# Second attention of a two-attention block: products in every second slot, feed-forward steps in the others

## What is computed

```python
x = x + attn_a(layernorm(x))     # 16 heads of 16; softmax over keys, summed: 'blmh,blhd->blhd'
x = x + ffn(layernorm(x))
x = x + attn_b(layernorm(x))
x = x + ffn(layernorm(x))

def attn_b(x):                   # the second attention
    q = (x @ Wq + bq).reshape(b, h, dh, t)      # dh = 16, t = 2048
    k = (x @ Wk + bk).reshape(b, h, dh, t)
    v = (x @ Wv + bv).reshape(b, h, dh, t)
    attn = softmax(einsum('bhdt,bhds->bhts', k, v) * temperature)   # over s
    return einsum('bhdt,bhts->bhds', q, attn).reshape(b, t, d)

def ffn(x):
    y = square(relu(x @ W_fc.T)) @ W_proj.T     # 256 -> 1024 -> 256
    # five steps of a spiking neuron on y; the result is the share of steps with a spike
```

## Time and profile before

| | before |
|---|---|
| median of 3 runs | 3005.08 (3004.95 to 3009.67) |
| the profiled execution | 3006.15, span 3003.9 |
| busy, TensorE / VectorE / ScalarE / GpSimd | 2439.2 / 2547.5 / 2552.0 / 1220.3 |
| mean granted clock of TensorE | 0.947 |
| reductions of the second attention (L805) | 1024, mean 1216 ns |
| exponentials of the second attention (L949) | 1024, mean 1119 ns |
| product matmuls (L560) | 4096 records, mean 605 ns |

### The profile page before, as it was taken

One profiled execution on the slowest core, in us unless ns is written; L12 is line 12 of the kernel. 1 busy time (PEld: TensorE's weight loads), 2 busy tenths in 40 slices (PEclk: granted clock), 3 DMA queues, 4 the chain that ended last, 5 costly groups with the idle time before them and its releaser, 6 DMA issues. The chain is left out here.

```text
span 3003.9 us, 47095 instructions
## 1 busy us (share of the span) xinstructions
PE 2439.2 (81%) x12608; PEld 1045.7 (35%) x12608; DVE 2547.5 (85%) x2612; ACT 2552.0 (85%) x4737; POOL 1220.3 (41%) x1856
## 2 busy tenths in 40 slices
PE   6832777777777777777776999999999999999997
PEld 3400334433334433334433233333333333333333
DVE  5552999999999999999983999999989988998994
ACT  2252999999999999999984999999999999999994
POOL 0000355554455554455543234443344334433444
PEclk9965999999999999999986999999999999999999
DMA  5897111111111111111111111101110111111100
GB/s 170 170 158 86 23 39 32 34 33 37 38 38 32 33 32 38 38 38 31 34 30 44 36 43 40 41 26 42 39 41 27 39 39 41 31 36 40 40 26 13
DMA packets 183490, 138.99 MB, mean 46 GB/s; under 512 B 91012, under 2 KB 170374, under 8 KB 183431
## 3 DMA queue, kind: packets, MB, share of 16 engines
q1 hardware_dynamic: 183430, 138.28, 20.1%
HBM read 92.04 MB, written 41.94 MB: 45 GB/s over the span
## 5 line engine op out<-in xcount | busy, mean ns | idle before, releaser
L805 DVE TENSOR_REDUCE nmax<-score 128x1 f32<-128x1024 f32 x1024 | 1214.1, 1216 | 165.9 <-PE score L580 149.0
L823 DVE TENSOR_REDUCE nmax<-score 128x1 f32<-128x1024 f32 x1024 | 1192.9, 1214 | 172.6 <-PE score L612 167.7
L949 ACT ACTIVATE big<-score,nmax 128x1024 f32<-128x1024 f32 x1024 | 1138.5, 1119 | 124.6 <-DVE nmax L805 118.0
L969 ACT ACTIVATE score<-score,nmax 128x1024 f32<-128x1024 f32 x1024 | 1118.6, 1098 | 127.5 <-DVE nmax L823 126.5
L612 PE MATMUL score<-big,shared 128*128 128x512 bf16 x2048 | 648.8, 406 | 370.8 <-ACT score L969 275.8
L580 PE MATMUL score<-shared 128*128 128x512 bf16 x2048 | 620.0, 390 | 103.7 <-ACT big L949 80.0
L560 PE MATMUL bank_g<-big,qw 128*32 128x512 f32 x4096 | 544.8, 605 | 2.3 <-POOL qw L1123 1.3
L612 PEld LDWEIGHTS score<-big,shared 128*128 128x128 bf16 x2048 | 135.6, 100 | 691.7 <-ACT score L969 549.1
L580 PEld LDWEIGHTS score<-shared 128*128 128x128 bf16 x2048 | 138.6, 98 | 650.0 <-ACT big L949 521.1
L1065 POOL TENSOR_TENSOR hid<-hid 128x512 f32<-128x512 f32 x128 | 133.0, 1039 | 509.0 <-ACT hid L915 509.0
L535 PEld LDWEIGHTS bank_f<-xnT,w_fc_sb 128*128 128x128 f32 x2048 | 295.1, 197 | 78.0 <-ACT hid L915 24.5
(11 more groups left out here) (113 smaller groups left out, 1606.0 us busy)
## 6 DMA issues: line engine op xcount, KB each, us to landing
shared<-q_parts SPq DMA_DIRECT2D x256, 64.0 KB, 3.1
shared<-kb_parts SPq DMA_DIRECT2D x256, 64.0 KB, 2.2
shared<-vb_parts SPq DMA_DIRECT2D x256, 64.0 KB, 2.2
big<-k_parts SPq DMA_DIRECT2D x32, 256.0 KB, 12.5
big<-k_parts SPq DMA_DIRECT2D x8, 1024.0 KB, 56.2
q_parts<-big SPq DMA_DIRECT2D x24, 256.0 KB, 3.1
k_parts<-big SPq DMA_DIRECT2D x24, 256.0 KB, 3.6
kb_parts<-shared SPq DMA_DIRECT2D x96, 64.0 KB, 1.5
```

The costliest lines, as they stand in the source:

```text
L805: v.tensor_reduce(nmax[:, par, c // NCH, c % NCH:c % NCH + 1], score[buffers_b[CPT * par + c][0]][:, :], AX.X, ALU.max, negate=True).then_ ...
L823: v.tensor_reduce(nmax[:, par, c // NCH, c % NCH:c % NCH + 1], score[buffers_a[CPT * par + c][0]][:, :], AX.X, ALU.max, negate=True).then_ ...
L949: a.activation(expo[:, c // NCH, (c % NCH) * CH:(c % NCH + 1) * CH], score[buffers_b[CPT * par + c][0]][:, :], ACT.Exp, bias=nmax[:, par, ...
L969: a.activation(s[:, :], s[:, :], ACT.Exp, bias=nmax[:, par, c // NCH, c % NCH:c % NCH + 1], accum_out=esum[:, par, c // NCH, c % NCH:c % N ...
```

## The change

The slots of phase_b are laid out anew: the products stand in every even slot, one feed-forward step in each odd slot from 3 on (two down steps in slot 31). ScalarE's copies and relus move with them, the copy of the product to the slot of the last product; VectorE's statistics go from slots 24 and 25 to 27 and 28, its last-tile neuron from 22 to 31. There are two qw tiles, so weigh_q waits for the half before the last. The exponentials wait for the products that free their rows at four slots instead of two. GpSimd's list has a new order, with the second square between half_distance and half_sums of half 0.

```diff
-UP_A, UP_B = [18, 19, 20, 21, 22, 23, 24, 25], [4, 4, 5, 5, 8, 11, 14, 14]
-DOWN_A, DOWN_B = [26, 26, 27, 27, 28, 29, 30, 30], [17, 18, 18, 19, 19, 20, 20, 21]
-PROD_AT = [6, 7, 9, 10, 12, 13, 15, 16], [22, 23, 25, 26, 28, 29, 31, 32]
+UP_A, UP_B = [18, 19, 20, 21, 22, 23, 24, 25], [3, 5, 7, 9, 11, 13, 15, 17]
+DOWN_A, DOWN_B = [26, 26, 27, 27, 28, 29, 30, 30], [19, 21, 23, 25, 27, 29, 31, 31]
+PROD_AT = [6, 8, 10, 12, 14, 16, 18, 20], [22, 24, 26, 28, 30, 32, 34, 36]
...
+E_FREE = [(0, 3), (6, HALF), (16, HALF + 4), (24, H)]
...
-        qw = sb("qw", [P, NCH, HALF, 2 * DH])
+        qw = sb("qw", [P, 2, NCH, HALF, 2 * DH])
...
-                    last = mm(bank_g[32 * sc:32 * sc + 32, :], qw[:, sc * BANK // CH, n, :],
+                    last = mm(bank_g[32 * sc:32 * sc + 32, :], qw[:, half, sc * BANK // CH, n, :],
...
-            v.memset(qw[:, :, :, :], 0.0).then_inc(consts, 1)
+            v.memset(qw[:, :, :, :, :], 0.0).then_inc(consts, 1)
...
-                        if c == 24:
+                        if c == 27:
                             ffn_stats_of(T + i1, 1 - par, x3_ready, i1 + 1)
-                        if c == 25:
+                        if c == 28:
                             ffn_mean(T + i1)
-                    if c == 22 and i2 is not None and last_tile(T + i2):
+                    if c == 31 and i2 is not None and last_tile(T + i2):
...
-                    need(act, prod_done, H * (i - 1) + HALF)
-                if c == CPT // 2:
-                    need(act, prod_done, H * i)
+                for at_c, n in E_FREE:
+                    if c == at_c:
+                        need(act, prod_done, H * (i - 1) + n)
...
-                    if i1 is not None and c == PROD_AT[0][-1] + 1:
+                    if i1 is not None and c == PROD_AT[0][-1]:
                         keep_product(i1)
                     if i2 is not None:
                         if c == 1:
                             ffn_columns(T + i2)
-                        if c == 4:
+                        if c == 8:
                             ffn_act(T + i2, 0)
-                        if c == 13:
+                        if c == 16:
                             ffn_act(T + i2, 1)
-                        if c == 20:
+                        if c == 30:
                             ffn_take(T + i2, par)
...
-                need(pool, prod_done, HALF * n)
+                need(pool, prod_done, HALF * (n - 1))
...
-                    last = g_.tensor_tensor(qw[:, c, :, 0:DH].rearrange("p (r m) j -> p r m j", m=KC),
+                    last = g_.tensor_tensor(qw[:, half, c, :, 0:DH].rearrange("p (r m) j -> p r m j", m=KC),
```

More of the change, by code:

```diff
@@ L1217, in phase_b @@
                     half_sums(i1, 1 - par, 1)
-                if i3 is not None:
-                    spikes(T + i3, T - 1 + i3, 1 - par, 7, 8)
                 if i1 is not None:
@@ L1222, in phase_b @@
                 if i3 is not None:
-                    spikes(T + i3, T - 1 + i3, 1 - par, 9, LIF_OPS)
+                    spikes(T + i3, T - 1 + i3, 1 - par, 1, 5)
                 if i2 is not None:
@@ L1226, in phase_b @@
                 if i3 is not None:
+                    spikes(T + i3, T - 1 + i3, 1 - par, 6, 7)
+                if i is not None:
+                    half_distance(i, par, 0)
+                if i2 is not None:
+                    square(T + i2, 1)
+                if i is not None:
+                    half_sums(i, par, 0)
+                if i3 is not None:
+                    spikes(T + i3, T - 1 + i3, 1 - par, 8, 8)
+                if i is not None:
+                    weigh_q(i, par, 0)
+                if i3 is not None:
+                    spikes(T + i3, T - 1 + i3, 1 - par, 9, LIF_OPS)
                     if isinstance(i3, int) and i3 < 2:
@@ L1230, in phase_b @@
                     result(T + i3, T - 1 + i3, 1 - par, out_stored[1 - par], 8 * (i3 - (1 - par)))
[L1231 to L1236, removed]
                 if i1 is not None:
                     add_attention(i1, 1 - par)
-                if i2 is not None:
-                    spikes(T + i2, T - 1 + i2, par, 1, 2)
-                if i1 is not None:
                     normalise(T + i1, 0, ffn_mv, ffn_step, xn[:, :], xin[:, 1 - par, :], ffn_tr, T + i1).then_inc(ffn_xn, 1)
-                if i2 is not None:
-                    spikes(T + i2, T - 1 + i2, par, 3, 6)
                 if i is not None:
```

## The result

| | before | after |
|---|---|---|
| median of 5 runs each, one chip | 3005.31 (3004.95 to 3009.67) | 3025.24 (3024.10 to 3028.96) |
| ratio after / before | | 1.0065 (1.0050 to 1.0079) |
| the profiled execution | 3006.15, span 3003.9 | 3027.4, span 3025.3 |
| copy of the product to the next copy, regular / with the turn-back | 42.03 / 42.49 | 42.97 / 43.35 |

The changed kernel is slower by 19.9, 0.65%. The forecast was slower, by 36.9, at 3042; 3025.24 lies in its range. In the kernel after, lines of phase_b stand two lower: scores L582, products L562, exponential L951, copy of the product L939, reciprocal L798, tot L1113, square L1067, xnT L911.

What follows compares the result with a forecast made beforehand. A ring of TensorE, ScalarE and VectorE was taken as the bound. 0.22 - 1.10 + 1.13 + 1.00 = +1.25 an iteration, mean 1.23 with the turn-back, 36.9 in thirty, gave 3042 by the median; range 3008 to 3053.

Steps and rivals of the forecast that it cites:

- P0 to P8: From the start of slot 0's score matmul (P) to slot 8's: 11.42 against 11.20 before, a loss of 0.22.
- Spacing the products: Products alternating with steps on TensorE: gain 1.10 an iteration in slots 8 to 17, loss 0.22 in slots 0 to 8.
- the release behind xnT: Slot 3's up step on TensorE, taken to start 0.60 after ScalarE's xnT copy starts, at 5.13.
- The square before the sums: GpSimd's second square ahead of half_sums: slot 18's reciprocal on VectorE waits 1.2, loss 1.13 an iteration.
- The copy of the product: Slot 22's product on TensorE waits 1.27 for ScalarE's copy after exponential 20, loss 1.00 an iteration.
- The floor of 1.0: Slot 22's wait for the copy would still be 1.0 if ScalarE stood as close to TensorE as it can.
- both waits: Main case: slot 18's reciprocal and slot 22's product both wait, 3034 to 3050, chance 0.62.
- the sums alone: Rival: only slot 18's reciprocal waits for tot, the copy is hidden: +0.6 an iteration, 3025, chance 0.10.
- clock unchanged: Sign expected in the profile after: the granted clock, 0.99 over the second attention's stretch, stays as it was.
- The ramp and the tail: Start and end of the second attention: ramp 0, between -2 and +1; tail 0, between -3 and +3.
- Neither new wait bites: Rival: in slots 18 to 23 copy and sums are in time: -0.43 an iteration, 2992, chance 0.12.
- The copy alone: Rival: only slot 22's product waits, GpSimd taking relu 1 early: +0.1 an iteration, 3009, chance 0.04.

Runs made afterwards that it cites:

- e2_sums_first: The changed kernel with GpSimd's half_sums of the first half ahead of the second square: 2998.39, ratio 0.9961.
- e9_all_but_slots: The kernel before with two qw tiles, the finer waits and GpSimd's new order, all slots as they were: 3005.63, ratio 0.9995.
- e1_copy_early: The changed kernel with ScalarE's copy of the product one slot earlier, after exponential 19 instead of 20: 3000.21, ratio 0.9966.
- e3_both: The changed kernel with the copy of the product one slot earlier and half_sums ahead of the second square: 2972.24, ratio 0.9876.
- a0_changed: The changed kernel itself, run once more on another chip: 3026.92, ratio 1.0058 to the kernel before.
- e4_both_xnt: The changed kernel with the product's copy one slot earlier, half_sums before the second square, and xnT copied after exponential 0 instead of 1: 2953.11, ratio 0.9812.
- e8_before_slot2: The kernel before with half 0's last product in slot 34 instead of 32, two qw tiles and the finer waits: 3000.78, ratio 0.9974.
- e10_before_xnt: The kernel before with only xnT copied after exponential 0 instead of 1: 3012.78, ratio 1.0006.
- e5_copy_late: The changed kernel with the copy of the product one slot later, after exponential 21 instead of 20: 3078.06, ratio 1.0228.

## Why the prediction was right in its sign and too large

By its own checkpoints, from the scores' starts above:

| stretch | before | predicted | after | predicted change | change |
|---|---|---|---|---|---|
| P0 to P8 | 11.20 | 11.42 | 11.32 | +0.22 | +0.12 |
| P8 to P18 | 13.15 | 12.05 | 12.06 | -1.10 | -1.09 |
| P18 to P22 | 4.96 | 6.09 | 6.00 | +1.13 | +1.04 |
| P22 to next P0 | 12.72 | 13.72 | 13.60 | +1.00 | +0.88 |
| iteration | 42.03 | 43.28 | 42.98 | +1.25 | +0.95 |

**Spacing the products** was right: the ten slots from 8 cost 12.06, in turns of 1.53 and 0.88. Slots 0 to 8 were over by 0.10, and the term that was off is the release behind xnT. Exponential 1 and xnT start 3.43 and 4.53 behind P0, exactly as in the working; the up step starts at 4.96 and not at 5.13. The two rows are, kernel before (TensorE) and kernel after (ScalarE):

```profile
2152.95 0.60 PE L580 MATMUL score<-shared 128*128 128x512 bf16 x2 [0.53 <-ACT big L949]
```
```profile
2162.10 0.37 ACT L911 ACTIVATE xnT<-bank_f 128x256 f32<-128x256 f32 x1
```

My 0.60 from xnT to the step (2152.79 to 2153.39) was no release: in the kernel before, TensorE was still waiting for slot 4 until 2152.95, and the step stands 0.44 behind those scores, which is the length of a score alone. In the kernel after, where TensorE does wait for xnT, it is 0.43 from start to start, 0.06 from the end of the copy. The transposes' slot is 0.69 (2159.09 to 2159.78) where I had 0.80, but that is not on the path: TensorE waits 0.60 in slot 3 all the same.

**The square before the sums** was right in mechanism and place, with 1.07 of idle for 1.2. The relu came 1.19 behind P18 and the square 0.66 behind the relu, where I had 1.23 and 0.70; that is the 0.09 of this stretch. e2_sums_first shows that it is this order, with the new slots, and e9_all_but_slots that it is not the order alone.

**The copy of the product** was right too. Its start came where it was put, 0.97 behind P22 (0.98 in the working), and the product 1.70 behind P22 for 1.80: without the wait it would start at 0.53, so by starts the wait is 1.17 for 1.27 (the record's 1.10 counts from the end of the scores). The step that was off is again the release: I took 0.23 from the copy's end to the product, out of the same misread row on xnT; it is 0.14 (2188.51 to 2188.65). The floor of 1.0 does not follow from my own prices, which give 1.90 + 1.92 - 1.53 - 0.88 - 0.54 = 0.87; e2_sums_first has 0.92 by starts (2176.32 - 2174.87 - 0.53).

**The sum** was mis-sized by a quarter: 0.90 for 1.23 on the mean of the two kinds of iteration (43.16 against 42.26), 27 for 36.9 in thirty. In the regular iteration 0.30 of it lies in three places, all on the same side: the release behind xnT 0.10, the reciprocal 0.09, the copy 0.12. So the 0.90 lies just under my 1.23 less 0.3, and the 3025.24 under the band for "both waits", 3034 to 3050; it is the very number that I gave to "the sums alone". The total could not have told the two apart. That it is both waits is shown by their rows and by e1_copy_early to e3_both, and that the total falls on 3025 is chance, in part the clock's (below).

**What the sum had no term for** is the clock of the kernel before. The earlier trace rows say 0.99 over the stretch, and I read 0.99 as full. Six turn-backs of 1.2 each lie in the missing hundredth, 7.1 of the 1273.4 between the first copy and the 31st. The change fills slots 2 and 4 with products, and none is long in its trace, nor in those of a0_changed and e1_copy_early to e4_both_xnt; that a product there is enough, e8_before_slot2 shows for slot 2. The balance in spans: from the first copy to the 31st 1293.2 against 1273.4, which is +26.8 for the iterations and -7.1 for the clock; +2.7 at the start (first copy at 1671.59 for 1668.89), -1.0 from the 31st copy to the end; together +21.4, as measured. The forecast that "clock unchanged" would be seen in the profile was wrong.

**The edits put at nothing** stayed at nothing: the second qw tile and the finer waits (e9_all_but_slots, with the old slots; with the new ones the view of waits has no entry for them), the statistics (no wait for x3_ready appears; copy to add is 2187.92 to 2194.82, 6.90 against 6.89). The ramp and the tail, put at 0, came to +2.7 and -1.0, the first outside its bound of +1 (a0_changed, the same kernel, has its first copy at 1673.42, so the start varies by more than a us of itself).

**The rivals.** "Neither new wait bites" had 2992, from -0.43 an iteration. Built as e3_both it is -0.87 and 2972.24, so the spacing is worth twice what I gave it. 0.10 of the difference is the release behind xnT; 0.23 is the stretch from P22 to the next P0, where e3_both takes 12.49 with products and steps in turn and the kernel before 12.72 with products in pairs, a gain that my working names nowhere. The last 0.1 is not taken apart. "The copy alone" had +0.1 an iteration and is -0.02 (e2_sums_first, mean 42.24), "the sums alone" had +0.6 and is +0.02 (e1_copy_early, mean 42.28). Against the spacing by itself that makes 0.85 for the copy and 0.89 for the sums, where my working had 0.53 and 1.03.

**Left open:** why only some of the turn-backs lose the clock, though the same waits stand at all of them (six in the trace of the kernel before, eight in e9_all_but_slots, eight and a regular iteration in e10_before_xnt), and what the wait at slot 8 (0.83), where the order of buffers turns, costs once the others are gone. None of these was tried.

## What to carry to other kernels

Spreading the work evenly over an engine's slots moves the last piece later, and with it everything that waits for the last piece: go through these consumers (the copy that frees the accumulator, the relu and what stands behind it on an in-order queue) and move each one by itself. Here the spreading was worth 0.87 an iteration and two such consumers took back 1.77; with each put one place earlier the same idea gives 2972 instead of 3025, and 2953 with xnT earlier too. Take the price of a release only from a row in which the engine waited for just that: the 0.60 behind xnT was TensorE waiting for something else. And a granted clock of 0.99 over a long stretch is worth looking into: it was six drops of 1.2 each.

## What was unexpected of the hardware

- A short thin stretch of TensorE costs more than its idle time. In the kernel before, waits of 1.35 and 0.53 ahead of two scores in a row were followed, at six of the turn-backs, by a granted clock of 0.57 over the next 4.0, at the price of 1.2; in e5_copy_late a wait of 2.23 behind one of 0.51 by 0.50 over 3.5, with intervals up to 47.34 instead of 44.50; in e10_before_xnt once 0.89 and 0.76 by 0.60. In the kernel after, 0.51 and 1.10 never did it, nor did 0.36 and 0.53 in e8_before_slot2.
- From the end of a copy on ScalarE to the matmul on TensorE that waits for it, 0.14 for the copy of the product and 0.06 for xnT (kernel after).
- Moving one activation by one slot moves a waiting engine by one whole exponential, 1.14 (e5_copy_late), or by the whole wait, 0.60 (e4_both_xnt). Both agree to 0.03 with a row of the changed kernel, the exponential of 1.11 and the wait of 0.60.
